# Attention on one core: the product with the inverse sums moves from VectorE to GpSimd, and the row maxima run six query tiles ahead

## The reference

```
x = x + conv_attention(group_norm(x))      # layer 0: 12 heads of 32 channels, rel. position biases
t = t + attention(layer_norm(t))           # layer 1: 12 heads of 32 channels, no biases
t = t + moe(layer_norm(t))                 # 8 experts, 2 per token
# for each head of an attention layer:
scores = q @ k.T * scale (+ rel_h + rel_w in layer 0)    # 1024 x 1024
out = softmax(scores, axis=-1) @ v
```

## Time and profile before

| | us |
|---|---|
| median of 3 runs | 1006.41 (1001.41 to 1008.95) |
| profiled execution, its time | 1002.1 |
| its span | 1000.3 |
| PE busy | 879.1 (88%) |
| DVE busy | 526.9 (53%) |
| POOL busy | 457.2 (46%) |
| ACT busy | 328.3 (33%) |
| mean granted TensorE clock | 0.945 of full speed |

### The profile page before, as it was taken

The page is one execution under the profiler, slowest core; times in us unless marked ns, Lnnn a source line. Parts: engine busy times, 40 slices in busy tenths (PEclk is TensorE's granted clock), DMA queues, the critical chain, the costliest instruction groups (busy, mean ns, idle before and its releaser), DMA issues.

```text
span 1000.3 us, 17750 instructions
## 1 busy us (share of the span) xinstructions
PE 879.1 (88%) x6029; PEld 641.9 (64%) x6030; DVE 526.9 (53%) x883; ACT 328.3 (33%) x582; POOL 457.2 (46%) x360
## 2 busy tenths in 40 slices
PE   4969899999998899999898978616999999999991
PEld 3457466566665444555454534516999999999991
DVE  4334767676776444878788772722233333233224
ACT  0212144554545222445454544201222322322230
POOL 0000076676778200346464665558076177077303
PEclk9989699999999999999999989957999999999996
DMA  9564723534424019335464571351356455455214
GB/s 291 109 147 150 271 76 87 130 104 110 127 84 154 11 32 231 92 84 176 127 206 126 195 241 37 125 185 49 115 179 219 145 174 197 167 181 176 87 32 141
DMA packets 74367, 139.23 MB, mean 139 GB/s; under 512 B 11000, under 2 KB 49080, under 8 KB 74320
## 3 DMA queue, kind: packets, MB, share of 16 engines
q1 hardware_dynamic: 62720, 120.42, 39.3%
q10 hardware_dynamic: 9552, 11.93, 3.6%
q0 software_dynamic: 2048, 6.29, 2.0%
HBM read 91.39 MB, written 43.55 MB: 135 GB/s over the span
## 4 chain that ended last, share of the span: by engine, by line
PE 43%; issue 8%; DVE 8%; POOL 6%; DMA 3%; ACT 1%; DVEq 0%; SPq 0%; POOLq 0%; ACTq 0%
PE ps L796 14%; PE ps L807 11%; DVE mhalf L891 4%; PE ps L628 4%; PE ps L585 3%; PE ps L603 3%; POOL qf L518 3%; PE ps L727 2%; PE ps L618 2%; POOL xs L547 1%; POOL gy L556 1%; PE ps L683 1%; DVE rec L901 1%; PE ps L778 1%; ACT prob L1074 1%
## 5 line engine op out<-in xcount | busy, mean ns | idle before, releaser
L891 DVE TENSOR_REDUCE mhalf<-ps 128x1 f32<-128x512 f32 x384 | 242.0, 679 | 95.6 <-PE ps L603 94.1
L1074 ACT ACTIVATE prob<-ps 128x1024 f32<-128x1024 f32 x192 | 190.5, 1026 | 186.7 <-PE ps L628 110.0
L518 POOL TENSOR_TENSOR qf<-qf,prob 128x1024 f32<-128x1024 f32 x84 | 206.1, 2453 | 18.2 <-POOL qf L518 8.1
L796 PE MATMUL ps<-xT,w 128*128 128x128 f32 x1440 | 166.8, 278 | 1.6 <-ACT xT L1146 1.4
L796 PEld LDWEIGHTS ps<-xT,w 128*128 128x128 f32 x1440 | 166.1, 194 | 2.1 <-issue 2.1
L603 PE MATMUL ps<-km,qm 96*128 96x512 f32 x384 | 145.3, 445 | 20.1 <-DVE mhalf L891 15.3
L618 PE MATMUL ps<-qa,ka 97*128 97x512 f32 x384 | 147.4, 426 | 8.6 <-DMA qa<-row 8.2
L1163 ACT ACTIVATE h_f<-ps,b1c 128x128 f32<-128x128 f32 x240 | 68.4, 368 | 215.6 <-PE ps L796 161.0
L603 PEld LDWEIGHTS ps<-km,qm 96*128 96x128 f32 x384 | 74.1, 194 | 71.5 <-DVE mhalf L891 51.9
L514 POOL TENSOR_TENSOR qf<-prob 128x1024 f32<-128x1024 f32 x24 | 57.1, 2379 | 134.7 <-ACT prob L1074 134.7
L628 PE MATMUL ps<-prob,va 128*32 128x256 f32 x1536 | 109.8, 393 | 0.0
(11 more groups left out here) (130 smaller groups left out, 874.5 us busy)
## 6 DMA issues: line engine op xcount, KB each, us to landing
w<-in_w SPq DMA_DIRECT2D x24, 768.0 KB, 7.4
w_raw<-in_w SPq DMA_DIRECT2D x24, 768.0 KB, 12.0
heads<-parts SPq DMA_DIRECT2D x56, 256.0 KB, 4.7
qa<-heads SPq DMA_DIRECT2D x24, 256.0 KB, 3.7
ka<-heads SPq DMA_DIRECT2D x24, 256.0 KB, 3.9
qb<-heads SPq DMA_DIRECT2D x12, 512.0 KB, 5.1
xs<-zero SPq DMA_DIRECT2D x8, 768.0 KB, 4.9
qm<-heads SPq DMA_DIRECT2D x12, 384.0 KB, 3.7
```

The costliest lines, as they stand in the source:

```text
L518: pool.tensor_tensor(acc[b], acc[b], prob[:, n % NP, :], ALU.add).then_inc(a_ok[L], 1)
L796: last = mm(ps[:, g, c % HG * P:(c % HG + 1) * P], w1[b][:, k, c * P:(c + 1) * P], xT[:, k, :], start=(k == 0), stop=(k == KT - 1))
L891: v.tensor_reduce(mhalf[:, b, qt, half:half + 1], max_bank(qt, half), AX.X, ALU.max).then_inc(mx_ok[L], 1)
L1074: act.activation(prob[:, s % NP, :], ps[:, 2 + 2 * (s % 2):4 + 2 * (s % 2), :].rearrange("p a b -> p (a b)"), ACT.Exp).then_inc(p_ok[L], 1)
```

## The change

The multiplication by the inverse sums moves to POOL. It stands there behind the last addition of the following head, and waits for the four pieces of the inverse. For the last head it comes right behind the output of the head before it. `AHEAD` becomes 6: step s of head g computes tile s + 6 of head g + 1 for s < 2, and tile s - 2 of head g + 2 from s = 2 on; turning the row, sending it and loading it each come one step earlier, since their places are written as TT - AHEAD and TT - AHEAD + 2. Head 0 of a layer has two tiles of maxima in its first step.

```diff
-AHEAD = 5
+AHEAD = 6
-MAXIMA_FIRST = [[(1, 5)], [(1, 6)], [(1, 7)], [(2, 0)], [(2, 1)], [(2, 2)], [(2, 3)], [(2, 4)]]
+MAXIMA_FIRST = [[(1, 5), (1, 6)], [(1, 7)], [(2, 0)], [(2, 1)], [(2, 2)], [(2, 3)], [(2, 4)], [(2, 5)]]
@@ gpsimd
+                def output(h, b):
+                    pool.wait_ge(o_rc[L], 4 * (h + 1))
+                    wait(pool, st_o[L][b], 32 * (h - b))
+                    pool.sem_inc(pool_in, 1)
+                    pool.tensor_tensor(osb[b][:], vsb[:, 0, :], rec[:], ALU.mult).then_inc(o_ok[L], 1)
+
-                def add_tiles(h, b, last=False):
+                def add_tiles(h, b, first=False, last=False):
...
                             pool.tensor_tensor(acc[b], acc[b], prob[:, n % NP, :], ALU.add).then_inc(a_ok[L], 1)
+                        if n == ADDS[L] and not first:
+                            output(h - 1, 1 - b)
+                    if last:
+                        output(h, b)
...
-                add_tiles(0, 0)
+                add_tiles(0, 0, first=True)
@@ vector
-                def output(h, b):
-                    wait(v, st_o[L][b], 32 * (h - b))
-                    v.wait_ge(o_rc[L], 4 * (h + 1))
-                    v.tensor_tensor(osb[b][:], vsb[:, 0, :], rec[:], ALU.mult).then_inc(o_ok[L], 1)
-
...
-                        if s == 6 and not first:
-                            output(h - 1, 1 - b)
...
-                output(NH - 1, 1)
```

## The result

The changed kernel takes 1035.6 us (median of 4 runs, 1032.2 to 1037.2) against 1004.8 us (4 runs, 1001.4 to 1009.0): a ratio of 1.030, 95% interval 1.025 to 1.035, slower. The profiled execution has a span of 1035.1 us against 1000.3. The forecast was slower by 20.6 us, 1023 with a range of 1006 to 1040; it is slower by 31, inside the range.

A forecast was written before the change was run, and what follows sets the result against it. Layer 0 was taken as near PE's limit at 17.6 us a head, layer 1 as delayed by DVE's output. Layer 0 +19.8, layer 1 0, ends +1.8, earlier turn -1.0 give +20.6 on 1002.1: 1023, range 1006 to 1040.

The forecast's parts named there:

- The mechanism: On SP, loads of q and k for the maxima queue behind the output's stores and reach PE late; layer 0 +19.8 us.
- T: Start of POOL's first addition in a head; T(g) is that start in head g.
- P0: Time of one head without PE's wait for q and k: 17.6 us in layer 0, 15.8 in layer 1.
- The fixed time of k: q and k usable by PE at T(g) + 22.6 us in layer 0, T(g) + 18.1 in layer 1.
- the clock's: Rival: TensorE's clock dips behind each second of 18 new waits, 7 to 13 us more, about 1033; chance 0.07.
- the prediction's own pairs: PE's waits in consecutive heads have a fixed sum, long then short: 5.1 us in layer 0, 2.8 in layer 1.
- Layer 1's period: 17.2 us a head before, 15.8 without DVE's output; 12.6 us saved and 12.6 of waits: 0 over nine heads.
- POOL's reserve: POOL takes an addition's fourth `prob` tile 2.9 us after it is ready; 3.3 us waits pass this by 0.4.
- third rival, POOL caught in the stall: Additions wait for `prob` tiles behind PE's stall, so each wait delays the output too: +56 us, 1059; chance 0.07.
- The starts of the layers: Extra tile of maxima at the start of a layer, missing again in head 10: 0 us.
- The stretches behind T(10): Ends of both layers: +1.8 us for POOL's last products, -1.0 for the earlier turn of the row.
- K2: Theory from the experiments: with VectorE's product behind maxima that stand behind PE's wait, each wait passes on in full.

The follow-up runs named there:

- the filler: The changed kernel plus eight extra PE multiplications of 512 columns ahead of its wait for q and k: 1024.6 us, ratio 1.021.
- the run with four multiplications: Kernel before with maxima six tiles ahead, product still on VectorE, and four extra PE multiplications ahead of its wait for q and k: 1021.3 us, ratio 1.017.
- the earlier product: The changed kernel with POOL's product behind the last but one addition, no longer behind the last: 1027.0 us, ratio 1.021.

## Why the prediction was right, and where its size was off

*The mechanism* holds: reordering SP's queue alone takes the loss and 8 us more away, and the waits for k with it. In head 4, the one before the long wait above, POOL's product ends at T + 14.1 (forecast 14.4) after 0.73 us (forecast 0.79); PE gets q and k at T(4) + 22.55, 231.67 - 209.12 (forecast 22.6). P0, which only the kernels without a wait can show, is 17.6 us in layer 0, as forecast. The loop adds up from what the traces show: 9 x 17.6 and 16.1 us of waits and 10.3 of clock are 184.8 of the 185.0 us of layer 0; 9 x 15.1, 11.8 and 10.2 are 157.9 for the 157.6 of layer 1.

*The fixed time of k did not hold in every head.* PE gets it between T + 21.2 and T + 24.5 in heads 1 to 8 of layer 0, and on average at 22.7. That the average is so near the forecast is luck: the output comes 0.7 us later than forecast (T + 15.1) and the way from there to PE takes 0.5 us less (7.7). Two waits in a row add up to 3.1 to 4.9 us, less than the forecast 5.1, since the dips lengthen the heads between them.

*The term that failed is the clock's.* It stood as a rival beside the forecast, with 0.07; but it is no rival, it comes with the forecast's own waits. In layer 0 PE's clock falls behind the waits of 2.08, 1.71, 3.15, 1.78 and 1.97 us and not behind those of 1.14, 1.37, 1.42 and 1.51. A dip lengthens the head, and on average the waits give half of it back, by the prediction's own pairs: (17.6 + 10.3 / 9 + 22.7) / 2 = 20.7 us a head; measured 20.6. Half of the 20.5 us lost in both layers is 10.3, and the filler gave back 11.0. That it is half is worked out, and by layers it fits less well (the filler took 7.3 us off layer 0 and about 4 off layer 1); that the dips cost something of that size, 9 us with a margin of 6, is shown. The waits themselves came out shorter for it: 16.1 us in layer 0, forecast 22.2.

*Layer 1's period was read too high.* The 17.2 us that I took for a head had three dips in it; the steady head is 16.7, and without the product on VectorE 15.1, not 15.8. So removing it is worth 1.6 us a head (forecast 1.4), the pair of waits has 3.5 us and not 2.8, and (15.1 + 10.2 / 9 + 18.6) / 2 = 17.4, measured 17.5. The two errors nearly cancel: +2.8 where 0 stood.

*POOL's reserve* of 2.9 us was set against the wait alone, and did not cover the dip behind it: the additions idled 10.3 us for ACT in layer 0. The prediction had named this as a sign of being wrong, and it is its third rival, POOL caught in the stall, in part: in the five heads with a dip (2, 3, 5, 6 and 8) the product ends at T + 15.0 to T + 17.0, in the other four at T + 13.9 to T + 14.1. The 1059 of that rival needs it in every head.

*The starts of the layers* were put at 0, "missing again in head 10". In layer 0 they have 4.8 us more. 1.2 is the second tile in the first step: PE takes 2.21 us for four multiplications where it took 1.05 for two, at the low clock; 1.8 is a longer wait for the first row of maxima (3.86 against 2.06), in front of the changed place; the rest is not accounted for. The stretches behind T(10), forecast +0.8, have 2.6. As single executions of unchanged code differ by as much here (T(0) of layer 0 lies between 123.7 and 126.2 us in the five traces with five tiles ahead), neither says much about the change. One term can be seen: the wait for the row in layer 1, 5.5 us in head 10, is gone, and T(10) to T(11) takes 2.3 us less there (forecast -1.0).

*The prediction's pairs need the product behind POOL's last addition.* The change has a merit that it did not name: since POOL takes the product behind its own additions, a wait of PE up to its reserve isn't passed on to the output. With the product on VectorE it is, by K2. That this is why six tiles ahead alone cost 25 us and not 10 is argued, with the waits in every head for it; a part of the difference is the clock (some 6 us by the run with four multiplications, no more than the scatter).

## What to carry to other kernels

Before an instruction moves, follow what its end releases down to the queue that waits for it: here a DMA queue of one order held the load for the next stage behind the store of this one, and an output 3 us later, on an engine that had room, with its load asked for 1.8 us earlier, became up to 3.15 us of a standing TensorE. Ask first whether the queue's order is needed; the change is worth 13 us with the loads ahead of the stores and costs 31 behind them. And price a new wait of TensorE with the clock that it loses behind it, and read the period of a loop from heads at full clock.

## What the runs showed of the hardware

The clock can fall behind a wait of 1.7 us between two stretches in which PE was busy (in layer 1 of the changed kernel behind one of 1.5), and stays at half for some 3.5 us, in places for 7 or 10. The length of the wait alone doesn't decide: with the earlier product, waits of 2.26 and 2.64 us had no dip behind them. In layer 1 of the kernel before, the same wait for DVE (1.74 us at the weight load, 1.1 to 1.3 us at the multiplication) had a dip behind it in three of nine heads; with a filler of four multiplications (1.1 us) in another place of the head, and six tiles ahead, the one profiled execution had none in layer 1. The Trainium skill (TensorE: Matmul & The Clock Gate, What's actually happening) has the clock fall with idling; the trace agrees in the direction, and shows how short a wait can be enough. The product of 128x256 values takes POOL 0.73 us in all 24 cases (0.724 to 0.740). VectorE took 0.43 to 2.63 us for it, depending on where it met POOL's additions. The Trainium skill (GPSIMD Engine Reference, 4.1 Engine selection) puts GpSimd at about twice VectorE's time for two inputs; here it is 0.73 us to the 0.43 that VectorE took where nothing stood in its way, 1.7.
